# The k projection of the first attention half a row later, with its split and its stacking

## The chip, the cores and the metric

The kernel runs on one core of a Trainium2 chip. The metric is the device time of one execution, in microseconds (us), as the median of several runs.

## What is computed

Four layers follow each other on 8 sequences of 1024 tokens with 256 features: a causal attention with a window of 128 tokens, a mixture of experts that picks tokens, a linear attention, and a second full attention. Each adds its input and normalises the sum. The change touches the first attention alone:

```
q = apply_rope(proj(Wq, bq)) * Dh ** (-0.5)
k = apply_rope(proj(Wk, bk))
v = proj(Wv, bv)
scores = einsum('bhqd,bhkd->bhqk', q, k)
blocked = (rel > 0) | (rel < -WINDOW)
probs = softmax(where(blocked, -inf, scores))
out = einsum('bhqk,bhkd->bhqd', probs, v)
x = layernorm(x + einsum('bsd,ed->bse', out, Wo) + bo)
```

with 16 heads of 16 features.

## The kernel before

The first attention works in 16 blocks of 4 tiles of 128 tokens. Its engines run one hand-written list of steps, `steps` (lines 358 to 372), once for each block B; a step `(offset, kind, i)` works for block B + offset. Every engine takes its own part of each step in the order of the list, so the list sets the order on all five engines at once.

A pass through the list has four **rows**, i = 0 to 3. A row has two halves, and each half is made by `merged` (line 142), which places the j-th of n steps of a stream at the key (j + 0.5) / n and sorts all streams by that key; on equal keys the earlier stream goes first.

- First half: four weightings `pv` (probabilities times V, line 710), four score steps `nat` (scores whose row maximum is wanted, lines 775 and 785), and what `begun[i]` names. VectorE (DVE) reduces each `nat` to row maxima (line 655). Then `oT`, a copy of the weighted sum by ScalarE (ACT, line 601).
- Second half: four transposed score steps `tr` (lines 775 and 785 again), each of which ACT turns into exponentials (line 590); `maxT` (PE turns the row maxima, line 791, and DVE casts them, line 659); `place` (ACT issues two DMAs that put the maxima in place, line 596); `back` (line 794; DVE takes reciprocals and multiplies, lines 662 and 664); and what `front[i]` names: the projections `q`, `k` (both line 752) and `v` (line 757), the output projection `proj` (line 803, summed by DVE at line 671), `aoT` (transposes, line 798, copied by ACT at line 604), and the parts of the layer norm: `statistics` (lines 176 and 182, with the root on GpSimd, POOL, at line 189) and `normalise` (line 195).

PE writes the results of all steps in `slotted` to three PSUM slots of 1024 columns in turn (`Schedule`, line 260). A step waits until the step three places ahead of it in that ring has been read. Steps that have no block to work for are left out of the ring, as near the end of the layer.

The way of k: PE projects it (line 752), DVE adds the bias and multiplies by the rotation's tables in four instructions (line 639), POOL subtracts and adds (lines 549 and 551), ACT casts the high part (line 583) and POOL takes the low part (line 557); this is `split k`. SP then writes both parts to DRAM (line 507), and `stack k` reads them back in stacked form with six DMAs (line 481). The first `nat` of row 1 in the next pass waits for all of them (`stacked`, lines 727 to 729). POOL has `bias` (line 545) in row 2, between these steps. In the queue of SP, `normalise` stores the finished block (line 525), behind a wait for DVE's line 195.

`lent` (line 374) lists steps that stand empty in the last block; the next layer uses their slots to turn its first input (line 957) and to set up tables (`memsets`). The k projection is one of them: at its place DVE copies a turned tile and runs three memsets.

Of the kernel before, what the change touches and what calls it, by code (L numbers as in the profile page):

```python
# [338 lines left out]
def window_attention_layer(nc, block, semaphores, x_in, y_out, wq_in, wk_in, bq_in, bk_in, wvT, bv_in, woT, bo_in, cos_in, sin_in,  # L339
# [15 lines left out]
    SCALE = float(DH) ** -0.5  # L355
    CH = D // P

    begun = {1: [(2, "split q", 0)], 2: [(2, "split k", 0)], 3: [(2, "stack k", 0)]}
    front = {0: [(-1, "aoT", 1), (2, "xT", 0), (2, "xT", 1), (2, "q", 0)],
             1: [(2, "k", 0), (0, "again", 0)],  # L360
             2: [(0, "bias", 0), (-1, "proj", 0), (-1, "statistics", 0)],
             3: [(-1, "normalise", 0), (0, "aoT", 0), (1, "v", 0)]}
    steps = [(3, "load", 0)]
    for i in range(BT):
        on, tn = divmod(i + 3, BT)
# [10 lines left out]
    with ExitStack() as ctx:  # L376
# [3 lines left out]
        def part(buffer, first, shape, dtype=f32):  # L380

            n = 1
            for size in shape[1:]:
                n *= size
            names = "abcd"[:len(shape) - 1]
            flat = buffer[0:shape[0], first:first + n]
            flat = flat.rearrange(f"p ({' '.join(names)}) -> p {' '.join(names)}", **dict(zip(names[1:], shape[2:])))
            return flat if dtype == f32 else flat.bitcast(dtype)
# [23 lines left out]
        aoT = part(out_place, (CH + 2 + BT) * D, [P, CH, BW])  # L412
# [1707 lines left out]
def four_layers(nc, x, wq, wk, bq, bk, wv, bv, wo, bo, cos, sin, mask, maskT, ident, ident16,  # L2120
                controller, f1, f2, f1_bias, tie, wqkv, wproj, bproj, head_blocks,
                q_w, q_b, k_w, k_b, v_w, v_b, o_w, o_b, norm_w, norm_b, out):

    def dram(name, shape):
        return nc.dram_tensor(name, shape, f32, kind="Internal").ap()

    x1, x2, x3 = (dram(f"x{i}", (NSEQ, T, D)) for i in (1, 2, 3))
    with ExitStack() as counting, ExitStack() as opened:
        semaphores = Semaphores(nc, counting)
        with nc.Block() as block:  # L2130
            with ExitStack() as kept:
                first, programs = token_choice_layer(nc, block, semaphores, kept, x1, x2, controller, f1, f2, f1_bias, tie, ident,
                                                     dram("expert_outputs", (2, 128, 32, D)))
                tail = window_attention_layer(nc, block, semaphores, x, x1, wq, wk, bq, bk, wv, bv, wo, bo, cos, sin, mask, maskT, ident,
                                              ident16, dram("qk_rows", (2, 2, 2, 16, 2, 8, T // 2)), first)
                spent = tail.spent
                with ExitStack() as ctx:
                    tail = programs(tail, *allocators(nc, ctx, semaphores, "l0f")[:2])
            opening = Opening(*allocators(nc, opened, semaphores, "opening")[::2])
            tail = linear_attention_layer(nc, block, semaphores, tail, opening, x2, x3, wqkv, wproj, bproj, ident, head_blocks)  # L2140
            nested_width_attention_layer(nc, block, semaphores, spent, tail, opening, x3, out, q_w, q_b, k_w, k_b, v_w, v_b, o_w, o_b,
                                         norm_w, norm_b, dram("kq_rows", (2, 2, D, T)))
# [58 lines left out]
```

How the kernel before makes its waits and increments, by code:

```python
def wait_alone(eng, sem, value):  # L63
    eng.wait_ge(sem, value)
    alone(eng)
# [37 lines left out]
    def wait(self, eng, block, n=None):  # L103
        eng.wait_ge(self.sem, self.count(block, n))
# [27 lines left out]
    def wait_free(self, pe, b, key):  # L133
        old = self.before(key)
        if old is not None:
            for sem, per_sequence, position in self.emptied(old):
                pe.wait_ge(sem, b * per_sequence + position)
# [44 lines left out]
    def reciprocal_root(self, pool, b, use):  # L184
        pool.wait_ge(self.aggregated, self.count(b, use) * self.tiles)
        pool.tensor_scalar(self.mv[:, :, 1], self.mv[:, :, 1], LN_EPS, None, ALU.add).then_inc(self.var_ready, 1)
        pool.wait_ge(self.var_ready, self.count(b, use))
        pool.tensor_tensor(self.rstd[:, :], self.mv[:, :, 1], self.half[:, :], ALU.pow).then_inc(self.rstd_ready, 1)
# [45 lines left out]
    def wait_memsets(self, eng):  # L235
        eng.wait_ge(self.setup, 3)
# [15 lines left out]
def negative_mean(pool, ln, to, sems, X):  # L252
    pool.wait_ge(ln.rstd_ready, X + 1)
    pool.tensor_tensor(to[:, :], ln.mv[:, :, 0], ln.rstd[:, :], ALU.mult).then_inc(sems[0], 1)
    pool.wait_ge(sems[0], X + 1)
    pool.tensor_scalar(to[:, :], to[:, :], -1.0, None, ALU.mult).then_inc(sems[1], 1)
# [43 lines left out]
    def use(self, pe, X, step, B):  # L301
# [5 lines left out]
        if i > -4 * size:  # L307
            for sem, count in self.until(B + i // size, self.plan[i % size]):
                pe.wait_ge(sem, count)
        return self.slot_in(B, step)
# [649 lines left out]
    def logits(pe, X, s):  # L960
        if X == 0:
            pe.wait_ge(consts, 16 * NCONST)
        xT_even.wait(pe, X)
```

## Time and profile before

| | us |
|---|---|
| median of 3 runs | 2532.25 |
| lowest and highest | 2531.35, 2538.84 |
| the profiled execution | 2531.27 |
| its span, first to last instruction | 2529.4 |
| first attention, in that span | about 0 to 1060 |

| engine | busy us | share |
|---|---|---|
| PE | 2190.4 | 87% |
| DVE | 1419.5 | 56% |
| ACT | 994.7 | 39% |
| POOL | 899.1 | 36% |

The shares are averages over four layers. For this change only the first 1060 us count, and within them the repeating pass of about 61.7 us. The timeline gives for each instruction, or group of merged instructions, the start, the length, the engine and line, and in brackets the idle time before it with what ended it. Work of PE overlaps a little: the next piece can start up to 0.1 us before the last one is over.

### The profile page before, as it was taken

How to read it: one execution, taken by the hardware profiler on the slowest of the kernel's cores; microseconds unless marked ns; L12 is line 12 of the kernel's file. 1: busy time of each engine (PE TensorE's matmuls, PEld its weight loads, DVE VectorE, ACT ScalarE, POOL GpSimd, SP SyncE). 2: the span in 40 equal slices, each digit the busy share in tenths (PEclk: the TensorE clock that was granted, in tenths of full speed). 3: DMA queues.
4: the chain of work that ended last, by engine and by line, in shares of the span. 5: the costliest groups of instructions: out<-in, count | busy, mean ns of one | idle time of the engine just before them, and what ended most of it. 6: DMA issues, size and time to landing. Idle time of an engine off the chain costs nothing.

```text
span 2529.4 us, 42561 instructions
## 1 busy us (share of the span) xinstructions
PE 2190.4 (87%) x17140; PEld 1376.5 (54%) x17140; DVE 1419.5 (56%) x2526; ACT 994.7 (39%) x1450; POOL 899.1 (36%) x573
## 2 busy tenths in 40 slices
PE   4899999999999999788878599999588888888885
PEld 2445555555555555566667456776355555555553
DVE  3545555555555555556466444554466777676772
ACT  1233333333333333545435144333144554554443
POOL 4222222222222220103123022201457877787784
PEclk7899999999999999999999899999799999999997
DMA  6555555555555554367877722201663455445411
GB/s 150 117 118 110 109 110 110 109 115 110 113 110 116 110 107 89 125 212 261 280 248 266 263 92 67 67 26 33 190 161 99 114 145 145 132 113 146 128 35 50
DMA packets 227971, 328.81 MB, mean 130 GB/s; under 512 B 14544, under 2 KB 167104, under 8 KB 227520
## 3 DMA queue, kind: packets, MB, share of 16 engines
q1 hardware_dynamic: 220784, 321.49, 48.4%
q10 hardware_dynamic: 6992, 4.60, 0.6%
q8 instruction: 137, 2.24, 0.4%
q14 instruction: 58, 0.48, 0.1%
HBM read 197.46 MB, written 127.93 MB: 129 GB/s over the span
## 4 chain that ended last, share of the span: by engine, by line
PE 57%; DVE 16%; POOL 7%; DMA 7%; ACT 5%; issue 4%; SPq 3%; ACTq 1%; POOLq 0%; DVEq 0%
PE l0a_slot L775 8%; PE l0a_slot L785 7%; PE l0a_O L710 5%; DVE l1f_rowmax L1972 4%; PE l1a_slot L1568 4%; PE l0a_slot L752 4%; POOL l1f_added L1849 4%; ACT l0f_f L590 2%; PE l0a_slot L757 2%; PE l1a_slot L1559 2%; PE l0a_slot L803 2%; POOL l1f_added L1851 2%; DVE l0f_hidden L655 2%; DMA l0f_f<-in_dram 2%; PE l1f_slot L2103 2%
## 5 line engine op out<-in xcount | busy, mean ns | idle before, releaser
L590 ACT ACTIVATE l0f_f<-l0a_slot 128x1024 f32<-128x1024 f32 (+1 forms) x256 | 248.3, 971 | 337.8 <-PE l0a_slot L775 189.0
L655 DVE TENSOR_REDUCE l0f_hidden<-l0a_slot 128x4 f32<-128x1024 f32 (+1 forms) x256 | 293.4, 1156 | 115.5 <-PE l0a_slot L785 112.5
L1921 ACT ACTIVATE l1f_probs<-l1f_slot 128x1024 f32<-128x1024 f32 x240 | 243.8, 1022 | 271.9 <-PE l1f_slot L2103 265.2
L1849 POOL TENSOR_TENSOR l1f_added<-l1f_probs 128x1024 f32<-128x1024 f32 x117 | 277.3, 2370 | 152.4 <-ACT l1f_probs L1921 152.4
L1972 DVE TENSOR_REDUCE l1f_rowmax<-l1f_slot 128x1 f32<-128x1024 f32 x240 | 287.2, 1216 | 65.6 <-PE l1f_slot L2094 64.9
L775 PE MATMUL l0a_slot<-l0f_hidden 128*128 128x512 bf16 (+1 forms) x1024 | 296.0, 374 | 13.3 <-DMA l0f_hl<-qk_rows 9.0
L549 POOL TENSOR_TENSOR l0f_x<-l0f_x 128x512 f32<-128x512 f32 x32 | 40.7, 1272 | 540.3 <-DVE l0f_x L639 540.3
L2103 PE MATMUL l1f_slot<-l1f_Qs,l1f_Ks 128*128 128x256 f32 x960 | 173.9, 306 | 39.0 <-DVE l1f_lo L1962 14.8
L2103 PEld LDWEIGHTS l1f_slot<-l1f_Qs,l1f_Ks 128*128 128x128 f32 x960 | 146.3, 198 | 96.9 <-DVE l1f_rowmax L1972 33.9
L2094 PE MATMUL l1f_slot<-l1f_Ks,l1f_Qs 96*128 96x512 f32 x480 | 175.9, 451 | 25.7 <-DVE l1f_rowmax L1972 18.4
L710 PE MATMUL l0a_O<-l0f_f,l0f_wide 128*32 128x128 f32 x3840 | 156.4, 279 | 10.5 <-issue 10.5
L1851 POOL TENSOR_TENSOR l1f_added<-l1f_added 128x512 f32<-128x512 f32 x117 | 149.6, 1279 | 9.2
L2027 PE MATMUL l1f_os<-l1f_probs,l1f_V 128*32 128x256 f32 x1920 | 145.4, 396 | 0.1
L785 PE MATMUL l0a_slot<-l0a_Qs,l0f_hl 49*128 49x256 f32 (+1 forms) x1024 | 127.1, 327 | 18.3 <-ACT l0f_f L590 17.1
L785 PEld LDWEIGHTS l0a_slot<-l0f_hl,l0a_Qs 48*128 48x128 f32 x1024 | 77.7, 188 | 103.8 <-issue 103.8
L785 PEld LDWEIGHTS l0a_slot<-l0a_Qs,l0f_hl 49*128 49x128 f32 x1024 | 76.8, 186 | 103.3 <-issue 68.3
L752 PE MATMUL l0a_slot<-l0f_x,l0f_spread 128*128 128x512 f32 x256 | 123.5, 629 | 6.6 <-DVE l0f_spread L623 5.1
L785 PE MATMUL l0a_slot<-l0f_hl,l0a_Qs 48*128 48x256 f32 (+1 forms) x1024 | 128.7, 330 | 0.0
L710 PEld LDWEIGHTS l0a_O<-l0f_f,l0f_wide 128*32 128x32 f32 x3840 | 90.3, 109 | 64.6 <-issue 37.4
L775 PEld LDWEIGHTS l0a_slot<-l0f_hidden 128*128 128x128 bf16 x1024 | 63.8, 98 | 96.5 <-issue 61.7
L2094 PEld LDWEIGHTS l1f_slot<-l1f_Ks,l1f_Qs 96*128 96x128 f32 x480 | 78.3, 199 | 68.8 <-issue 30.0
L601 ACT COPY l0f_f<-l0a_O 128x512 f32<-128x512 f32 x64 | 37.4, 585 | 196.1 <-PE l0a_O L710 196.0
(194 smaller groups left out, 3770.2 us busy)
## 6 DMA issues: line engine op xcount, KB each, us to landing
expert_outputs<-l0f_wide SPq DMA_DIRECT2D x64, 512.0 KB, 3.3
l0f_wide<-expert_outputs SPq DMA_DIRECT2D x32, 1024.0 KB, 10.9
l1f_Ks<-kq_rows SPq DMA_DIRECT2D x48, 512.0 KB, 8.2
l0a_Qs<-qk_rows SPq DMA_DIRECT2D x90, 256.0 KB, 7.8
l0f_hl<-qk_rows SPq DMA_DIRECT2D x90, 256.0 KB, 14.5
l0f_f<-in_dram SPq DMA_DIRECT2D x10, 2048.0 KB, 14.7
qk_rows<-l0f_wide SPq DMA_DIRECT2D x32, 512.0 KB, 2.8
qk_rows<-l0f_x SPq DMA_DIRECT2D x32, 512.0 KB, 4.2
```

Source lines behind the costliest of these rows:

```text
L590: exp_ready.by(act.activation(probs[:, t % 2, HG * g:HG * g + HG, 0:reach, :], s[:, :, 0:reach, :], ACT.Exp, scale=SCALE))
L655: max_ready.by(dve.reduce_max(rowmax[:, t, :, 2 * g:2 * g + 2], s[:, :, :, first:2 * P], AX))
L710: last = mm(O[t % 2][32 * j:32 * j + 32, g, :], V[:, tile - a, HG * g + j, :], probs[:, (t - a) % 2, HG * g + 2 * (j % 2) + j // 2, a, :], ...
L752: last = mm(s[:, BW * r:BW * r + BW], w[:, c, P * r:P * r + P], xT[:, n, c, :], start=c == 0, stop=c == CH - 1)
L775: at_end = mm(o[:, half, :, reach, :], ident16[:, :], table[:, reach, :].unsqueeze(1).broadcast_to([P, 2, wide, P]), start=not mask_ends, ...
L785: last = mm(o[:, half, j, reach, :].rearrange("p a q -> p (a q)"), left[r, 2 * g + j, here], right[r, 2 * g + j, moving], start=mask_ends ...
L1849: halved.by(pool.tensor_tensor(added[:, u, :], probs[:, 0, u, :], probs[:, 1, u, :], ALU.add))
L1851: add_done.by(pool.tensor_tensor(added[:, u, 0:SKT * QW], added[:, u, 0:SKT * QW], added[:, u, SKT * QW:HKT * QW], ALU.add))
L1921: exp_done.by(act.activation(probs[:, half, u - FIRST[b], :], s[:, :], ACT.Exp, scale=SCALE))
L1972: max_done.by(dve.reduce_max(rowmax[:, i:i + 1], s[:, :], AX))
L2094: last = mm(s[:, 512 * half:512 * half + 512], Qs[0:96, parity, u, P * t:P * t + P], Ks[0:96, parity, UNITS[u][0], 512 * half:512 * half + ...
L2103: last = mm(s[:, QW * j:QW * j + QW], Ks[:, parity, UNITS[u][0], P * kt:P * kt + P], Qs[:, parity, u, :], start=True, stop=True)
```

## The change

```
-    begun = {1: [(2, "split q", 0)], 2: [(2, "split k", 0)], 3: [(2, "stack k", 0)]}
+    begun = {1: [(2, "split q", 0)], 2: [(2, "k", 0)]}
     front = {0: [(-1, "aoT", 1), (2, "xT", 0), (2, "xT", 1), (2, "q", 0)],
-             1: [(2, "k", 0), (0, "again", 0)],
-             2: [(0, "bias", 0), (-1, "proj", 0), (-1, "statistics", 0)],
-             3: [(-1, "normalise", 0), (0, "aoT", 0), (1, "v", 0)]}
+             1: [(0, "again", 0)],
+             2: [(0, "bias", 0), (2, "split k", 0), (-1, "proj", 0), (-1, "statistics", 0)],
+             3: [(-1, "normalise", 0), (2, "stack k", 0), (0, "aoT", 0), (1, "v", 0)]}
```

The k projection moves from the second half of row 1 to the first half of row 2 (the third row), `split k` from the first to the second half of row 2, and `stack k` from the first to the second half of row 3. Since `merged` places a stream's steps by their number, the streams of rows 2 and 3, now of four steps each, also put their other steps elsewhere: `proj` comes after the third `tr` instead of the second; `normalise` comes ahead of `maxT`; `aoT` comes after the third `tr`; and `v` comes behind the fourth `tr`, as the last step of the pass.

**DVE, rows 1 and 2.** Line 639 with `l0a_bk` is the taking of k, line 655 reduces a `nat`, line 659 casts the maxima. Before:

```order
L639 SCALAR_TENSOR_TENSOR l0f_x<-l0a_slot2,l0a_bk,l0f_spread 128x512 [waits l0a_lo_ready,l0a_hi_ready,l0a_filled3]
L639 SCALAR_TENSOR_TENSOR l0f_x<-l0a_slot2,l0a_bk,l0f_spread 128x512 x3
L662 RECIPROCAL l0f_hidden<-l0a_slot2 128x16 [waits l0a_filled1]
L664 TENSOR_TENSOR l0f_f2<-l0a_slot2,l0f_hidden 128x256 [waits l0a_recip_ready]
L655 TENSOR_REDUCE l0f_hidden<-l0a_slot1 128x2x2 [waits l0a_filled2]
L655 TENSOR_REDUCE l0f_hidden<-l0a_slot2 128x2x2 [waits l0a_filled2]
L655 TENSOR_REDUCE l0f_hidden<-l0a_slot0 128x2x2 [waits l0a_filled2]
L655 TENSOR_REDUCE l0f_hidden<-l0a_slot1 128x2x2 [waits l0a_filled2]
L659 CAST l0f_hidden<-l0a_slot0 16x128 [waits l0a_placed1,l0a_filled2]
```

Now:

```order
L662 RECIPROCAL l0f_hidden<-l0a_slot1 128x16 [waits l0a_filled1]
L664 TENSOR_TENSOR l0f_f2<-l0a_slot1,l0f_hidden 128x256 [waits l0a_recip_ready]
L655 TENSOR_REDUCE l0f_hidden<-l0a_slot0 128x2x2 [waits l0a_filled2]
L655 TENSOR_REDUCE l0f_hidden<-l0a_slot1 128x2x2 [waits l0a_filled2]
L639 SCALAR_TENSOR_TENSOR l0f_x<-l0a_slot2,l0a_bk,l0f_spread 128x512 [waits l0a_lo_ready,l0a_hi_ready,l0a_filled3]
L639 SCALAR_TENSOR_TENSOR l0f_x<-l0a_slot2,l0a_bk,l0f_spread 128x512 x3
L655 TENSOR_REDUCE l0f_hidden<-l0a_slot0 128x2x2 [waits l0a_filled2]
L655 TENSOR_REDUCE l0f_hidden<-l0a_slot1 128x2x2 [waits l0a_filled2]
L659 CAST l0f_hidden<-l0a_slot0 16x128 [waits l0a_placed1,l0a_filled2]
```

The taking of k stands between the second and the third reduction of row 2, where it stood ahead of row 1's `back`.

**PE, end of row 3.** Line 798 is `aoT`, 794 is `back`, 757 is `v`, lines 775 and 785 are a `tr`, 710 is the first weighting of the next pass. Before:

```order
L798 MATMUL l0a_slot1<-l0f_ident,l0f_f2 128x128 [waits l0a_exp_ready,l0a_ao_ready]
L798 MATMUL l0a_slot1<-l0f_ident,l0f_f2 128x128 x3
L775 MATMUL l0a_slot2<-l0f_hidden 128x512 [waits l0a_maxT_ready]
L775 MATMUL l0a_slot2<-l0f_hidden 128x512
L785 MATMUL l0a_slot2<-l0a_Qs,l0f_hl 128x256 x4
L794 MATMUL l0a_slot0<-l0f_ident,l0f_f2 128x128 [waits l0a_exp_ready,l0a_oT_ready]
L794 MATMUL l0a_slot0<-l0f_ident,l0f_f2 128x128 x3
L757 MATMUL l0a_slot1<-l0f_spread,l0f_x 128x256 [waits l0a_aoT_ready]
L757 MATMUL l0a_slot1<-l0f_spread,l0f_x 128x256 x7
L785 MATMUL l0a_slot2<-l0a_Qs,l0f_hl 128x256 [waits l0a_exp_ready]
L785 MATMUL l0a_slot2<-l0a_Qs,l0f_hl 128x256 x3
L775 MATMUL l0a_slot2<-l0f_hidden 128x512 x2
```

Now:

```order
L775 MATMUL l0a_slot1<-l0f_hidden 128x512
L785 MATMUL l0a_slot1<-l0a_Qs,l0f_hl 128x256 x4
L798 MATMUL l0a_slot2<-l0f_ident,l0f_f2 128x128 [waits l0a_maxT_ready,l0a_ao_ready]
L798 MATMUL l0a_slot2<-l0f_ident,l0f_f2 128x128 x3
L794 MATMUL l0a_slot0<-l0f_ident,l0f_f2 128x128 [waits l0a_exp_ready,l0a_oT_ready]
L794 MATMUL l0a_slot0<-l0f_ident,l0f_f2 128x128 x3
L785 MATMUL l0a_slot1<-l0a_Qs,l0f_hl 128x256 [waits l0a_exp_ready]
L785 MATMUL l0a_slot1<-l0a_Qs,l0f_hl 128x256 x3
L775 MATMUL l0a_slot1<-l0f_hidden 128x512 x2
L757 MATMUL l0a_slot2<-l0f_spread,l0f_x 128x256 [waits l0a_aoT_ready]
L757 MATMUL l0a_slot2<-l0f_spread,l0f_x 128x256 x7
L710 MATMUL l0a_O0<-l0f_f1,l0f_wide 32x128 [waits l0a_oT_ready,l0a_v_ready,l0a_exp_ready]
```

`v` has changed places with the last `tr`, and two of the `tr` steps now use slot 1 with only `aoT` and `back` between them.

**DVE, row 3.** Line 195 is `normalise`, line 659 the cast of the maxima that `place` waits for. Before:

```order
L655 TENSOR_REDUCE l0f_hidden<-l0a_slot0 128x2x2 [waits l0a_filled2]
L659 CAST l0f_hidden<-l0a_slot2 16x128 [waits l0a_placed0,l0a_filled2]
L195 TENSOR_SCALAR l0f_x<-l0f_x,l0a_ln_mv,l0a_ln_rstd 128x256 [waits l0a_ln_rstd_ready]
L195 TENSOR_SCALAR l0f_x<-l0f_x,l0a_ln_mv,l0a_ln_rstd 128x256 x3
L662 RECIPROCAL l0f_hidden<-l0a_slot0 128x16 [waits l0a_filled1]
L664 TENSOR_TENSOR l0f_f2<-l0a_slot0,l0f_hidden 128x256 [waits l0a_recip_ready]
L647 TENSOR_TENSOR l0f_wide<-l0a_slot1,l0f_f2 128x16x16 [waits l0a_pv_done,l0a_filled2]
```

Now:

```order
L655 TENSOR_REDUCE l0f_hidden<-l0a_slot0 128x2x2 [waits l0a_filled2]
L195 TENSOR_SCALAR l0f_x<-l0f_x,l0a_ln_mv,l0a_ln_rstd 128x256 [waits l0a_ln_rstd_ready]
L195 TENSOR_SCALAR l0f_x<-l0f_x,l0a_ln_mv,l0a_ln_rstd 128x256 x3
L659 CAST l0f_hidden<-l0a_slot2 16x128 [waits l0a_placed0,l0a_filled2]
L662 RECIPROCAL l0f_hidden<-l0a_slot0 128x16 [waits l0a_filled1]
L664 TENSOR_TENSOR l0f_f2<-l0a_slot0,l0f_hidden 128x256 [waits l0a_recip_ready]
L647 TENSOR_TENSOR l0f_wide<-l0a_slot2,l0f_f2 128x16x16 [waits l0a_pv_done,l0a_filled2]
```

`normalise` stands ahead of the cast. On SP's queue, in words: the store of the finished block (line 525) now stands ahead of the six stacking DMAs of k, and was behind them.

## Rows read from the trace of the kernel before

**Rows 1.** Busy time in stretches: start:end, length, PE, PEld, DVE, ACT, POOL, clock, DMA.
```profile
60.00:121.70 61.70, 54.11 (x321) 25.92 (x319) 30.61 (x39) 15.47 (x17) 11.96 (x8) 0.86 0.65 131
...
430.00:491.60 61.60, 57.29 (x504) 31.25 (x500) 34.02 (x54) 20.91 (x26) 13.37 (x9) 1.00 0.56 112
```

**Rows 2.** Waits of PE, us 121.7 to 1007.3: total us, times, longest us.
```profile
PE l0a_slot L785 <- ACT l0f_f L590: 15.4, 29, 1.1
PE l0a_slot L791 <- DVE l0f_hidden L655: 15.0, 37, 0.6
PE l0a_slot L794 <- DVE l0f_x L639: 14.0, 13, 1.1
PE l0a_O L710 <- issue: 9.3, 15, 1.1
```

**Rows 3.** Timeline, PE, rows 1 and 2: start, length, instructions, idle before.
```profile
419.80 3.60 PE L752 MATMUL l0a_slot<-l0f_x,l0f_spread 128*128 128x512 f32 x8
...
426.31 0.63 PE L794 MATMUL l0a_slot<-l0f_ident,l0f_f 128*128 128x128 f32 x4 [1.07 <-DVE l0f_x L639]
...
435.42 0.28 PE L791 MATMUL l0a_slot<-l0f_ident,l0f_hidden 128*16 128x128 f32 x1 [0.63 <-DVE l0f_hidden L655]
...
475.35 0.65 PE L710 MATMUL l0a_O<-l0f_f,l0f_wide 128*32 128x128 f32 x16
475.93 0.60 PE L775 MATMUL l0a_slot<-l0f_hidden 128*128 128x512 bf16 x2
...
476.90 0.64 PE L710 MATMUL l0a_O<-l0f_f,l0f_wide 128*32 128x128 f32 x16
```

**Rows 4.** Timeline, PE, row 3 and the next block's start.
```profile
449.42 0.28 PE L791 MATMUL l0a_slot<-l0f_ident,l0f_hidden 128*16 128x128 f32 x1 [0.35 <-DVE l0f_hidden L655]
...
451.89 0.66 PE L794 MATMUL l0a_slot<-l0f_ident,l0f_f 128*128 128x128 f32 x4
452.68 3.72 PE L757 MATMUL l0a_slot<-l0f_spread,l0f_x 128*128 128x256 f32 x16
...
457.95 0.43 PE L710 MATMUL l0a_O<-l0f_f,l0f_wide 128*32 128x128 f32 x8 [0.59 <-issue]
```

**Rows 5.** Timeline, DVE, rows 3, 0 and 1.
```profile
448.14 1.22 DVE L655 TENSOR_REDUCE l0f_hidden<-l0a_slot 128x4 f32<-128x1024 f32 x1 [0.32 <-PE l0a_slot L785]
449.74 0.28 DVE L659 CAST l0f_hidden<-l0a_slot 16x128 fp32r<-16x128 f32 x1 [0.37 <-PE l0a_slot L791]
449.94 1.36 DVE L195 TENSOR_SCALAR l0f_x<-l0f_x,l0a_ln_mv,l0a_ln_rstd 128x256 f32<-128x256 f32 x4
...
456.44 1.41 DVE L647 TENSOR_TENSOR l0f_wide<-l0a_slot,l0f_f 128x256 f32<-128x256 f32 x4 [3.13 <-PE l0a_slot L757]
...
473.91 2.73 DVE L639 SCALAR_TENSOR_TENSOR l0f_x<-l0a_slot,l0a_bq,l0f_spread 128x512 f32<-128x512 f32 x4 [4.38 <-PE l0a_slot L752]
476.56 4.77 DVE L655 TENSOR_REDUCE l0f_hidden<-l0a_slot 128x4 f32<-128x1024 f32 x4
```

**Rows 6.** Timeline, ACT and its DMA queue, row 3.
```profile
450.70 1.02 ACT L590 ACTIVATE l0f_f<-l0a_slot 128x1024 f32<-128x1024 f32 x1 [0.57 <-PE l0a_slot L775]
450.71 1.29 ACTq L596 DMA_DIRECT2D l0a_Qs<-l0f_hidden  x2
452.04 0.58 ACT L604 COPY l0f_f<-l0a_slot 128x512 f32<-128x512 f32 x1 [0.31 <-issue]
```

**Rows 7.** Timeline, SP's queue, row 3; then landing times of line 481's transfers.
```profile
446.50 3.77 SPq L481 DMA_DIRECT2D l0f_hl<-qk_rows  x6
451.38 0.36 SPq L525 DMA_DIRECT2D x<-l0f_x  x1
...
DMA to landing us min/median/max: 4.5/11.2/18.1
```

**Rows 8.** Timeline, PE, last two blocks of the first attention.
```profile
973.23 0.50 PE L785 MATMUL l0a_slot<-l0a_Qs,l0f_hl 49*128 49x256 f32 x4 [0.49 <-ACT l0f_f L590]
...
1033.24 0.38 PE L775 MATMUL l0a_slot<-l0f_hidden 128*128 128x256 bf16 x2 [1.90 <-DVE l0f_f L664]
```

## The prediction

> **What bounds the kernel now.** I read the busy time in stretches first. In the settled part of the first attention PE is busy 57.29 of 61.60 us at a granted clock of 1.00, DVE 34.02, ACT 20.91, POOL 13.37 [rows 1]. So PE sets the time of a pass of the step list, and only what makes PE idle can be won or lost: about 4.3 us a pass. The waits of PE say where these are [rows 2]. Four kinds carry nearly all: PE waits for ACT's exponentials (15.4 us in 29 waits), with `maxT` for DVE's row maxima (15.0 in 37), with `back` for the taking of k (14.0 in 13), and at the first weighting (9.3 in 15; the page says "issue", but line 710 there waits for V, and DVE's line 647 ends just before it). Then I read the timeline around these places. The same pass comes back 14 times almost to the tenth, so one instance stands for all.
>
> The reader is to see one more thing in the timeline: work that ends a wait is covered only by the PE work that stands between. The change moves one step on purpose and several others by the rule of `merged`, so each wait has to be worked out anew from what now stands ahead of it.
>
> **Row 1: the wait behind k goes.** Before, k ends at 423.40, DVE takes it for 2.73 us, PE fills only two `tr` in that time and then `back`, which uses the slot of k, sits idle 1.07 us [rows 3]. Without k in that row, `back` uses the slot of `maxT`, whose cast is over long before. The `tr` steps behind `maxT` then wait for exponentials of the one two places ahead at the earliest; ACT needs 1.02 us for one [rows 6] and PE 0.97, with `maxT` or `back` between, so nothing is left over. k stands in 14 settled passes (blocks 0 to 13): **-1.07 x 14 = -15.0 us**.
>
> **Row 2: `maxT` waits longer.** k now ends between the second and third `nat`. I take its follow-up from q, which DVE takes at the start of a row in the same way: 2.73 us from 473.91, then four reductions in 4.77, so 1.19 each when they queue [rows 5]. Two of them make 2.4, and `maxT` can start about 0.05 + 2.7 + 2.4 + 0.05 = 5.2 us after k ends. In that time PE has two weightings and two `nat` of 1.55 together (475.35 to 476.90) of which the weighting is 0.58 (475.35 to 475.93) [rows 3], and one `tr` of the same 0.97: 3.1 + 0.97 = 4.07. The idle time is 1.14 where it is 0.35 in a usual row [rows 4]. In every second pass the `tr` is a narrow one, about 0.8; there it is 1.3 against 0.63 [rows 3]. So +0.79 and +0.68 in turn, **7 x 0.79 + 7 x 0.68 = +10.3 us**. The POOL and ACT parts of k (1.27 twice, a cast of 1.04, 2.35 for the low part, with 2.36 of `bias` now ahead of it) run while PE does the third `tr` and `proj`, 3.5 us, and nobody waits for them; I cost them at nothing. Without that cover they would cost at most the cast, 1 us a pass. `proj` behind the third `tr` moves DVE's sum and statistics about 1 us towards the next row; its first reduction starts some 0.7 us late and DVE, with 1.22 of work for every 1.55, has caught up by the third. Nothing again.
>
> **Row 3: V comes too late for the next weighting.** Before, `v` ends at 452.68 + 3.72 = 456.40, DVE starts at 456.44 and is done at 457.85, and the weighting starts at 457.95, 1.55 after the end of `v`; the last `tr` covers 0.96 of it and 0.59 is idle [rows 4, 5]. Now `v` is the last step and covers nothing: the whole 1.55 is idle, 0.96 more. `v` exists in 16 passes: **16 x 0.96 = +15.4 us**.
>
> **Row 3: the last `tr` waits for an exponential.** It uses the slot of the `tr` before it, with only `aoT` and `back` between. The same four steps (`maxT`, two `tr`, `aoT`) stand ahead of `back` as before, so `back` still runs from 451.89 to 452.55 [rows 4]. ACT is what has changed. It has to issue `place` between the exponentials, and `place` waits for the cast of the maxima, which now stands behind `normalise` on DVE: reduction to 449.36, `normalise` 1.36, cast 0.28, so 451.00 [rows 5]. The two DMAs take 1.29 and the next ACT instruction started 0.04 behind them [rows 6]: 452.34, then the exponential from 452.4 to 453.4, and the last `tr` at 453.45. That is 0.9 us idle, against 0.13 ahead of `v` before (452.55 to 452.68 [rows 4]): +0.77 in 14 passes, **+10.8 us**. If ACT does not let `place` hold it up, its end is 0.35 sooner and the term is +0.42 x 14 = 5.9; if the slot is free in time after all it is -0.13 x 14 = -1.8. I take the 0.77, since the rows show ACT's next instruction waiting for the DMA's end.
>
> **The two ends of the layer.** In the last blocks k, q and xT have nothing to do. Before, two `tr` of block 14 share a slot because k's place between them is empty: 0.49 idle, which goes. In the last block DVE runs the memsets at k's place and PE waits 1.90 for the `back` behind them; half a row later they lie beside `proj` and cost nothing [rows 8]. **-2.4 us**. At the start PE fills and waits in long stretches, at 0.86 of its clock in the first passes [rows 1]; I see no price there, and allow 3 us either way.
>
> **The sum** is -15.0 + 10.3 + 15.4 + 10.8 - 2.4 = +19.1 us against the profiled execution of 2531.27, so 2550.4. The median of the runs is 1.0 above that execution, so **2551 us**, 0.75% slower.
>
> **Rival 1: the smaller price.** `place` and the slot in row 3 cost nothing: without the +10.8 and with -1.8 it is 2532.25 + 6.5 = 2539. For it speaks that a few tenths of drift between ACT and PE decide; against it that ACT's chain adds up to nearly 1 us more than PE has to do. The decision point is an exponential that ends before 452.55.
>
> **Rival 2: faster.** Only the removed waits count (-15.0, -2.4) and the new places of `v`, `maxT` and the last `tr` are absorbed: 2532.25 - 17.4 = 2515. That needs PE to have later work that it may do first; the order shows PE's queue as a fixed list in which the weighting waits for V, so little speaks for it.
>
> **Rival 3: the stacked k lands too late.** SP's store waits for `normalise` (issued at 451.38) and now stands ahead of the six DMAs of k, which were issued from 446.50 on [rows 7]. They start 5 us later at least, at about 452, and are read by the first `nat` of row 1, some 0.6 after q's end at 473.9, or 2 us later in the new pass: 24 us. The longest landing is 18.1 us [rows 7]. Half of the queue ahead of them (q's share) will be further along, so I expect landings of no more than 18. Beyond a margin of 6 us each further microsecond costs 14 us; with 3 of them it is 2551 + 42 = 2593. The Trainium skill ("DMA: Bandwidth & Descriptors", section on queues, rings and completion order) says that each DMA engine consumes the descriptors of one queue in ring order; by that rule the 512 KB of the store also go ahead of k. The landing times of 18.1 us against an issue of 3.77 us for six agree with a queue that is worked off in turn.
>
> **Rival 4: the clock falls.** With some 1.4 us more idle time in a pass, and two waits close together in row 3, the granted clock could leave 2.4 GHz for stretches. In the early pass at a mean of 0.86, PE is at the lower level for 28% of 61.7 us and does 8.6 us less work at full speed [rows 1]. Were each pass to lose as much, it would be 2551 + 14 x 8.6 = 2671. Against it: the waits of today, 4.3 us a pass with single ones of 1.07, leave the clock at 1.00 [rows 1, 3]. The Trainium skill ("TensorE: Matmul & The Clock Gate", section on PSUM-queue depth-cycling) tells of a kernel whose clock swung because PE was idle for short times between groups while it turned through its PSUM banks. This kernel turns through three slots with waits of that kind, and its rows at 1.00 so far do not show it.
>
> **How the numbers follow.** A measurement of this kernel can tell about 0.3% from no change, 7.6 us. My forecast has 0.77, rival 1 with its kin (one of the three costs in rows 2 and 3 missing) 0.11, rival 2 0.05, rival 3 0.05, rival 4 0.02. Rival 1 at 2539 counts as no change. The range takes the forecast with its bounds (the `tr` term between 5.9 and 12, `maxT` 3 us either way, the start 3) and reaches to rival 1: 2539 to 2561. Faster 0.05, within 0.3% 0.12, slower 0.83.
>
> **What would show it.** In the profile after: no wait of line 794 for line 639; `maxT` of row 2 waiting 1.1 to 1.3 us; the first weighting of a pass waiting 1.5; line 785 of row 3 waiting 0.9 for line 590; a pass of about 63.1 us in place of 61.7; PE's clock still 1.00; no wait for the stacking. It is wrong if the pass is 61.7 or less, or if the stacked k or the clock appears among the causes.

## The result and the profile after

| | before | after |
|---|---|---|
| median, us | 2531.8 | 2571.55 |
| lowest and highest | 2530.9, 2538.84 | 2562.66, 2573.58 |
| the profiled execution | 2531.27 | 2573.58 |
| its span | 2529.4 | 2571.7 |

The changed kernel takes 1.0139 times as long (95% interval 1.012 to 1.0159), 39.8 us more by the medians. The forecast was 2551 with a range of 2539 to 2561: the direction was right, the loss is twice what was forecast and lies outside the range. Two single executions further down (3104 and 3491 us) ran at a much lower clock from start to end, and the medians given are those of the other executions.

The two spans, cut at the first and the sixteenth `v` and at the first turned tile of the second layer. The columns are start:end, length, busy time and count of PE, PEld, DVE, ACT and POOL, then clock and DMA. Before:

```profile
0.00:83.86 83.86, 46.96 (x142) 20.95 (x142) 35.40 (x37) 9.55 (x11) 33.49 (x18) 0.76 0.65 152
83.86:1002.06 918.20, 857.38 (x7682) 470.02 (x7680) 487.67 (x773) 323.41 (x386) 189.74 (x127) 1.00 0.54 107
1002.06:1058.39 56.33, 45.90 (x499) 30.21 (x500) 28.14 (x46) 24.26 (x29) 5.42 (x4) 0.98 0.40 139
1058.39:2529.40 1471.01, 1240.15 (x8820) 855.34 (x8820) 868.32 (x1672) 637.49 (x1025) 670.41 (x425) 0.94 0.46 142
```

After:

```profile
0.00:87.94 87.94, 50.27 (x148) 22.61 (x149) 36.84 (x37) 10.58 (x12) 33.53 (x18) 0.72 0.64 147
87.94:1041.63 953.69, 869.70 (x7681) 477.63 (x7680) 480.45 (x774) 321.59 (x385) 189.78 (x127) 0.98 0.52 104
1041.63:1096.35 54.72, 44.93 (x495) 29.46 (x493) 27.51 (x44) 23.38 (x28) 5.26 (x4) 1.00 0.37 128
1096.35:2571.70 1475.35, 1235.94 (x8820) 853.49 (x8820) 866.37 (x1672) 637.74 (x1025) 671.01 (x425) 0.94 0.47 142
```

Of the 42.3 us between the spans, 35.5 lie in the passes (953.69 - 918.20), 4.1 ahead of the first `v`, -1.6 behind the last, and 4.3 in layers whose code is the same. In the passes PE is idle for 84.0 us in place of 60.8, **+23.2**, and it is busy for 869.7 in place of 857.4 with as many instructions, **+12.3**. The forecast had the first of these two numbers and not the second.

The waits of PE after, from 121.7 to 1030 us (total us, times, longest), beside the same rows of before [rows 2]:

```profile
PE l0a_slot L785 <- ACT l0f_f L590: 31.8, 43, 1.2
PE l0a_slot L791 <- DVE l0f_hidden L655: 24.0, 36, 1.3
PE l0a_O L710 <- issue: 21.8, 14, 1.6
```

The row of line 794 behind line 639 is gone (-14.0). Line 785 has 16.4 more, line 791 9.0 more, line 710 12.5 more: +23.9 in all. The same places in the timeline of PE, one narrow pass, beside [rows 3, 4]:

```profile
452.27 0.28 PE L791 MATMUL l0a_slot<-l0f_ident,l0f_hidden 128*16 128x128 f32 x1 [1.30 <-DVE l0f_hidden L655]
...
468.65 0.60 PE L794 MATMUL l0a_slot<-l0f_ident,l0f_f 128*128 128x128 f32 x4
470.41 0.50 PE L785 MATMUL l0a_slot<-l0a_Qs,l0f_hl 49*128 49x256 f32 x4 [1.16 <-ACT l0f_f L590]
...
471.28 3.62 PE L757 MATMUL l0a_slot<-l0f_spread,l0f_x 128*128 128x256 f32 x16
476.46 0.42 PE L710 MATMUL l0a_O<-l0f_f,l0f_wide 128*32 128x128 f32 x8 [1.56 <-issue]
```

And where PE is busy for longer. The pass that follows, PE's timeline behind `maxT` of row 2:

```profile
515.60 0.28 PE L791 MATMUL l0a_slot<-l0f_ident,l0f_hidden 128*16 128x128 f32 x1 [1.02 <-DVE l0f_hidden L655]
515.81 0.50 PE L785 MATMUL l0a_slot<-l0a_Qs,l0f_hl 49*128 49x256 f32 x4
516.25 1.61 PE L775 MATMUL l0a_slot<-l0f_hidden 128*128 128x512 bf16 x4
517.78 0.79 PE L785 MATMUL l0a_slot<-l0a_Qs,l0f_hl 49*128 49x256 f32 x4
518.50 4.43 PE L803 MATMUL l0a_slot<-l0f_f 128*128 128x256 f32 x16
```

and the same stretch in windows (columns as above, the clock third from the end):

```profile
512.00:516.00 4.00, 2.98 (x33) 1.47 (x33) 3.63 (x5) 1.61 (x2) 3.91 (x3) 1.00 0.00 0
516.00:520.00 4.00, 4.00 (x16) 2.20 (x15) 0.20 (x1) 2.88 (x3) 1.88 (x2) 0.57 0.01 2
520.00:524.00 4.00, 4.00 (x24) 3.16 (x22) 1.02 (x1) 0.00 (x0) 1.42 (x1) 1.00 0.42 155
```

About one microsecond behind the end of a wait of 1.02 the granted clock goes from 2.4 to 1.2 GHz (the mean of 0.57 over 4 us puts the change at 516.6), stays there for about 3.4 us, and the four instructions that took 0.50 take 0.79. In windows of 2 us the trace of after has seven such **falls** between 130 and 1030 us: at 137, 196 (a long one, 7 us), 517, 544, 773, 838 and 967. Each begins within 2.0 us of the end of a wait that the change made: five behind `maxT` of row 2 (1.02 or 1.30), one behind the wait of 1.14 of line 785, one behind the 1.55 at the first weighting. Summed as (1 - clock) x length, which I call the **shortfall**, they come to 13.7 us. The trace of before has none there, in 15 waits of 1.02 and more.

### The profile page after: what moved, and what is told of

Read it like the earlier page. It is cut to its first block, busy times and chain, and to the rows that moved or that the text cites. A ratio compares the mean times of both kernels' runs of the same rounds, so it can differ in the third digit from the quotient of the medians.

```text
span 2571.7 us, 42561 instructions
## 1 busy us (share of the span) xinstructions
PE 2200.8 (86%) x17140; PEld 1383.2 (54%) x17140; DVE 1411.2 (55%) x2526; ACT 993.3 (39%) x1450; POOL 899.6 (35%) x573
## 4 chain that ended last, share of the span: by engine, by line
PE 56%; DVE 15%; DMA 7%; POOL 7%; ACT 6%; issue 4%; SPq 3%; ACTq 1%; POOLq 0%; DVEq 0%
PE l0a_slot L775 8%; PE l0a_slot L785 7%; PE l0a_O L710 5%; DVE l1f_rowmax L1972 4%; PE l1a_slot L1568 4%; PE l0a_slot L752 4%; POOL l1f_added L1849 4%; ACT l0f_f L590 4%; DMA l0f_f<-in_dram 2%; PE l0a_slot L803 2%; PE l0a_slot L757 2%; DVE l0f_hidden L655 2%; PE l1a_slot L1559 2%; POOL l1f_added L1851 2%; PE l0f_slot L1274 2%
```

## The experiments

The kernels below place single steps at keys of their own. `merged` got a second list for it, and with the keys of before or after it gives their order again:

```
def merged(*streams, at=()):
    ...
    keyed += [(key, 9, step) for key, step in at]
```

In the expectations `maxT` and `tr` go by the number of the step: "row 1's `maxT`" is step `maxT` 1, which stands in row 2. "Passes" is the time from the first to the sixteenth `v` in the trace. The medians of before differ from chip to chip (2534 to 2537 here, 2531.8 above), so each forecast is best read against the before of its own chip.

**k, its split and its stacking alone** (the keys of the other steps as before).

```
-    begun = {..., 2: [(2, "split k", 0)], 3: [(2, "stack k", 0)]}
+    begun = {..., 2: [(2, "k", 0)]}
+    front: 1: 0.5 again;  2: 1/6 bias, 0.375 split k, 0.5 proj, 5/6 statistics
+           3: 1/6 normalise, 0.375 stack k, 0.5 aoT, 5/6 v
```

> k, its split and its stacking stand where the change puts them; bias, proj, statistics, normalise, aoT and v keep the places of before. Theory A (the loss is idle time of PE that the neighbours' new places cause, and a clock that falls where such waits follow each other): the wait behind k goes (-15.0 us), the wait of maxT in row 2 stays at 1.0 to 1.3 us (+10 us), row 3 is as before, so 2522 to 2532 us, and the clock falls in one or two passes at most. Theory B (moving k itself, its DMAs above all, is what costs): it stays near 2565.

Measured: 2534.96 against 2535.59 of before on that chip, ratio 0.9995 (0.9978 to 1.0011). The wait behind k is gone, line 791 waits 24.4 us in 37 in place of 15.0, and PE's idle time in the passes falls from 60.8 to 55.3; one fall of the clock, behind a `maxT` wait of 1.30 at 804, takes 1.7 back. The row of line 785 stays at 16.3 us in 30, so neither k nor its stacking beside row 3 makes the wait of the last `tr`. The median lies 3 us above the stated 2522 to 2532, on a chip where before is 3 us slower too. What the change's title names costs nothing that can be measured, and theory A holds.

**Row 3 alone** (k where it was, row 3 as the change has it).

```
-             3: [(-1, "normalise", 0), (0, "aoT", 0), (1, "v", 0)]}
+             3: 0.125 normalise, 0.375 stack k, 0.625 aoT, 0.875 v
```

(`stack k` leaves the first half of row 3 for it.)

> Before with only row 3 of the change: stacking of k in its second half, normalise ahead of maxT, aoT behind the third tr, v last; k and its split where they were before. Theory A: the last tr waits 1.16 us instead of 0.13, and the first weighting 1.56 instead of 0.59, so 14 x 1.03 + 16 x 0.97 = +30 us from the waits, 2562 us, and more where the clock falls. Theory B: about 2532, since k is not moved.

Measured: 2569.59, 34.0 more than before on that chip where some 30 were expected, ratio 1.0131 (1.0104 to 1.0158). Its waits:

```profile
PE l0a_slot L785 <- ACT l0f_f L590: 31.5, 43, 1.2
PE l0a_O L710 <- issue: 21.8, 14, 1.6
PE l0a_slot L794 <- DVE l0f_x L639: 15.1, 14, 1.1
```

Nearly the whole loss is here, by two waits that the k projection itself has nothing to do with: `stack k` is a fourth step in `front[3]` and pushes the three others off their keys (in the next two kernels `v` and `normalise` are told apart). Two falls, both behind a wait of 1.56, add 3.4.

**`v` last alone** (before, with the key of `v` from 5/6 to 0.9).

> The kernel before with one step in another place: v of the next block behind the last tr of row 3, not ahead of it. By the sum on record the wait behind v grows from 0.59 to 1.55 (0.96 in 16 passes, +15.4); the last tr, no longer behind v, comes 3.5 us earlier and waits for its slot if ScalarE's copy is not done. Theory A (aoT's and stack k's place costs nothing of itself): 2547 to 2552 with no wait of the last tr, up to 2568 with a wait of 1.2 there as in the kernel with row 3 alone. Theory B (stack k beside it makes the last tr's wait): 2547 to 2552. What tells them apart is the row of L785 behind ScalarE's L590: 15.4 us in 29 waits as before for B, 31 in 43 for A.

Measured: 2555.59 against 2536.89, +18.7, ratio 1.0085 (1.0063 to 1.0107). Line 710 waits 23.4 us in 15, up to 1.6, and line 785 still 15.4 in 29. So `v` behind the last `tr` costs its 0.97 a pass in idle time, and the last `tr`'s wait is not its doing. That much is theory B; that `stack k` itself makes the wait, as B puts it, is not what the next kernel shows. Here the last `tr` uses the slot of `aoT` and waits 0.2 us in all for its copy. Three falls, behind waits of 1.56 at 462.5, 527.2 and 779.6, add 5.1 us of shortfall.

**The cast ahead of `normalise`** (after, `normalise` from 0.125 to 0.17).

> The changed kernel with normalise behind row 3's maxT, where the kernel before has it, and all else as changed. VectorE then casts maxT first. If the last tr waits for ScalarE, whose copies stand behind what VectorE gives it, the wait of 1.16 becomes about 0.8 and the kernel some 5 us faster than the changed one: 2564 to 2568; fewer stretches at the lower clock would add up to 5. If ScalarE's own work between sets that wait, nothing moves: 2570 to 2573. By neither does the wait behind v (1.56) change.

Measured: 2569.58, ratio 1.0134 (1.0118 to 1.015), no faster than after. But the wait is shorter, as expected. ACT and its queue in row 3, first in the kernel after, where VectorE's cast ends at 467.53:

```profile
467.56 1.66 ACTq L596 DMA_DIRECT2D l0a_Qs<-l0f_hidden  x2
469.33 1.02 ACT L590 ACTIVATE l0f_f<-l0a_slot 128x1024 f32<-128x1024 f32 x1 [0.91 <-issue]
```

and with the cast first:

```profile
465.50 1.29 ACTq L596 DMA_DIRECT2D l0a_Qs<-l0f_hidden  x2
466.89 1.02 ACT L590 ACTIVATE l0f_f<-l0a_slot 128x1024 f32<-128x1024 f32 x1 [0.37 <-issue]
...
467.97 0.51 PE L785 MATMUL l0a_slot<-l0a_Qs,l0f_hl 49*128 49x256 f32 x4 [0.62 <-ACT l0f_f L590]
```

The last `tr` waits 0.62 for 1.16, line 785 in all 24.1 us for 31.8. This shows the chain that the prediction named (cast, two DMAs of `place`, exponential, `tr`). The 0.62 that is left belongs to the new place of `aoT`: the last `tr` uses the slot of the `tr` before it, whose exponential ends at 467.91. Of the 7.7 us, 5.1 came back as clock in this trace: eight falls, 18.8 us of shortfall in place of 13.7, so that the passes are 4.1 us shorter and not 9; the later layers took 5.4 us longer in this execution. The stated 2564 to 2568 was missed for that.

The two DMAs took 1.29 us here and 1.66 in after, and SP's queue shows a difference beside them. In after they start with the stacking of k:

```profile
467.42 0.36 SPq L525 DMA_DIRECT2D x<-l0f_x  x1
467.88 4.29 SPq L481 DMA_DIRECT2D l0f_hl<-qk_rows  x6
```

With the cast first they begin 1.1 us ahead of SP's line 481 (466.63). In row 3 of after and of row 3 alone, all 25 such pairs lie beside 1.5 us or more of SP's DMA issuing and take 1.7 us; with the cast first and with k alone, all 26 lie beside 0.5 us of it and take 1.3. That the issuing of SP holds up that of ACT is likely by this, and was not tested by itself.

**The first `nat` of row 0 ahead of the first weighting** (after, streams exchanged).

```
-        steps += merged([... "pv" ...], [... "nat" ...], begun.get(i, []))
+        steps += merged(nats, pvs, begun.get(i, [])) if i == 0 else merged(pvs, nats, begun.get(i, []))
```

> The changed kernel with row 0's first nat ahead of its first pv, so that the nat (0.9 us of TensorE work that needs no V) covers the wait for VectorE's V. If V's arrival is what the idle behind v is, it falls from 1.56 to about 0.6: 0.95 in 14 to 16 passes, 15 us, and fewer falls of the clock, up to 7 more: 2549 to 2558. Rival: nat waits itself there for a slot or for the stacked k or q, and the idle only moves: 2566 to 2574. A second rival: ScalarE and VectorE, which then get row 0's work in another order, hold up the rest of the row: 2575 to 2590.

Measured: 2560.76, ratio 1.0098 (1.0082 to 1.0115). Line 710 waits 9.7 us in 14, longest 0.7, in place of 21.8, so it is V that the first weighting waits for. The passes are 12.2 us shorter than after, all of it idle time; there are still seven falls, now all behind the 1.30 of `maxT`. So the gain in the passes is the wait's own 12, without the fewer falls that the stated 2549 to 2558 counted on. All seven waits of 1.30 have a fall behind them here, six of seven with the cast first, and one of seven with k moved alone: the length of the wait does not decide by itself.

**All three waits filled with short matmuls** (after).

```
+            def busy(X, count, o, times):
+                oT_ready.wait(pe, X, count)
+                for m in range(times):
+                    mm(O[o][:, 0:2, :], ident16[:, :], mask[:, :, :], start=True, stop=True, ...)
...
+                if kind == "maxT" and i == 1 and 1 <= B < NBLOCK - 2:
+                    busy(X - 1, 2, 1, 5)
+                if kind == "tr" and i == NHG - 1 and 1 <= B < NBLOCK - 1:
+                    busy(X - 1, 3, 0, 6)
...
+                if kind == "v" and 1 <= B < NBLOCK - 1:
+                    busy(X - 1, 3, 0, 8)
```

> The changed kernel, with short bf16 matmuls of 256 columns written ahead of the three waits that the change made longer: 5 ahead of row 1's maxT, 6 ahead of row 3's last tr, 8 behind v (into bank halves of O that are free there; no result is read). At 0.11 us each (256 columns at 2.4 GHz) they are 0.5, 0.6 and 0.9 us in waits of 1.3, 1.2 and 1.6, so they should end before the wait does and cost nothing by themselves. Theory A (waits of one microsecond and more, close together, let the clock fall, and that is what the sum of the waits lacked): each wait in the trace is shorter by what was written into it, no stretch at 0.5 of the clock between 130 and 1000 us, and the 12.6 us that those stretches cost in the profiled passes are gone: 2556 to 2562. Theory B (the falls have another cause, or cost nothing of their own): the falls stay, 2568 to 2576. If TensorE's own time in these matmuls is longer than I reckon, the passes grow by the excess, at most 2600.

Measured: 2562.25, ratio 1.0101 (1.0082 to 1.012); its interval overlaps that of after only at the very edge. One narrow pass of its trace (line 700 is the filling; the others moved down by nine):

```profile
448.23 0.72 PE L700 MATMUL l0a_O<-l0f_hidden 128*128 128x256 bf16 x5
449.60 0.28 PE L800 MATMUL l0a_slot<-l0f_ident,l0f_hidden 128*16 128x128 f32 x1 [0.65 <-DVE l0f_hidden L655]
...
472.07 1.04 PE L700 MATMUL l0a_O<-l0f_hidden 128*128 128x256 bf16 x8
473.79 0.43 PE L719 MATMUL l0a_O<-l0f_f,l0f_wide 128*32 128x128 f32 x8 [0.68 <-issue]
```

The filling and the wait that is left are 1.37 together (0.72 + 0.65) where the wait was 1.30, and 1.72 (1.04 + 0.68) where it was 1.56: no useful work is added or taken away. Undisturbed passes are 62.57 and 64.15 us, as in after (62.55 and 64.15). Yet the passes take 943.4 in place of 953.7, because six of the seven falls are gone: theory A. The one that is left is a long one and begins at 134, behind the `maxT` of block 0, which was left unfilled:

```profile
133.15 0.28 PE L800 MATMUL l0a_slot<-l0f_ident,l0f_hidden 128*16 128x128 f32 x1 [1.02 <-DVE l0f_hidden L655]
133.35 0.50 PE L794 MATMUL l0a_slot<-l0a_Qs,l0f_hl 49*128 49x256 f32 x4
133.79 1.61 PE L784 MATMUL l0a_slot<-l0f_hidden 128*128 128x512 bf16 x4
```

An earlier filling, with 24, 28 and 36 f32 matmuls of 128 columns at the same waits, decides nothing:

> The changed kernel with small extra matmuls into the free accumulator at the three long waits (24 ahead of maxT in row 2, 28 ahead of the last tr, 36 behind v; 16 of this kind take 0.58 us in a weighting), so that PE works where it was idle and no step starts later. Theory A with the clock: the stretches at the lower clock go from blocks 1 to 14, and it is 12 to 17 us faster than the changed kernel, 2554 to 2560. Theory without a clock (the whole 40 us are waits): it is the same as the changed kernel or slower, 2571 or more.

Measured: 2648.34, ratio 1.0427 (1.039 to 1.0464). The trace has two records for each of these f32 matmuls (48, 56 and 72), and they lasted up to 2.8 us, longer than the waits. Beside that six new waits of 2.3 to 4.5 us came, about 140 us apart and in the middle of a weighting (line 717):

```profile
570.18 0.43 PE L717 MATMUL l0a_O<-l0f_f,l0f_wide 128*32 128x128 f32 x8
575.12 0.66 PE L717 MATMUL l0a_O<-l0f_f,l0f_wide 128*32 128x128 f32 x8 [4.52 <-issue]
```

No other engine works in most of that time (ACT's last exponential is over at 561.25, VectorE's reduction at 571.5). What PE waits for there stays open; the DMA queue of instructions carries 156 packets in place of the 137 of after.

**One kind of wait filled.** First only the wait behind `v` (the last two added lines above):

> The changed kernel with only the 8 short matmuls behind v (1.04 us of the wait of 1.56 in the trace with all three waits filled); row 1's maxT still waits 1.30 and the last tr 1.16. Theory A: the falls behind maxT stay, 4 to 7 of them, 2566 to 2572. Rival (the longest wait makes the falls): none or one is left, 2556 to 2563.

Measured: 2572.48, ratio 1.0153 (1.013 to 1.0176). Five falls, as theory A had it: three behind `maxT` waits of 1.30 and 1.02, one behind the `maxT` of block 0, one at 157 behind the one 1.56 that stands ahead of the first filled block. Then only `maxT` (the first two added lines):

> The changed kernel with only the 5 short matmuls ahead of row 1's maxT (0.72 us of its wait of 1.30 in the trace with all three waits filled); the last tr's 1.16 and the 1.56 behind v stay idle. Theory A (a fall of the clock follows one long wait, and the wait of row 1's maxT is the one that starts most of them, as it is in the trace with nat first): 2 to 4 falls are left between 130 and 1030 us, those behind v, as in the kernel with v last alone (3): 5 us of shortfall in place of 13.7, 2561 to 2566. Rival (the falls need the wait behind v, the longest): 6 or 7 falls stay, 2569 to 2575.

Measured: 2568.02, ratio 1.0135 (1.0115 to 1.0154). The mean clock of its trace is 0.64, in which single falls can't be seen. The same kernel once more:

> The same kernel as the one with only row 1's maxT filled, whose profiled execution was disturbed and told nothing of its falls. With all three waits filled one fall was left, with only the wait behind v filled five, all but one of them right behind a maxT's wait of 1.30. Theory A (the 1.30 of maxT starts most falls): 1 to 3 falls between 130 and 1030 us, with a shortfall of 2 to 5 us, and 2561 to 2568. Rival (any of the three long waits will do, so that it takes all three to be filled): 4 to 7 falls, now behind the waits of 1.56 and 1.16, and 2568 to 2574.

Measured: 2565.27, ratio 1.0119 (1.0097 to 1.0142). Three falls, two of them long, 8.6 us of shortfall: one behind the unfilled `maxT` of block 0, the two others behind waits of 1.56. One of these, with the windows from 596 to 608:

```profile
599.47 0.43 PE L717 MATMUL l0a_O<-l0f_f,l0f_wide 128*32 128x128 f32 x8 [1.56 <-issue]
...
601.15 0.91 PE L782 MATMUL l0a_slot<-l0f_hidden 128*128 128x512 bf16 x2
602.00 0.79 PE L792 MATMUL l0a_slot<-l0f_hl,l0a_Qs 48*128 48x256 f32 x4
```

```profile
596.00:600.00 4.00, 2.44 (x18) 1.63 (x17) 1.42 (x4) 0.00 (x0) 0.00 (x0) 1.00 1.11 207
600.00:604.00 4.00, 4.00 (x30) 1.40 (x28) 2.39 (x2) 0.00 (x0) 0.00 (x0) 0.66 1.07 153
604.00:608.00 4.00, 4.00 (x21) 1.46 (x20) 1.90 (x3) 0.59 (x1) 0.00 (x0) 0.50 1.08 155
```

Whichever wait is filled, no fall is left behind it, and the waits left open still have some. Theory A was right on the number of falls (1 to 3) and the time, and wrong on the shortfall (2 to 5 us); that the falls left stand behind waits of 1.56 is what the rival said.

**`v` earlier, and both steps where their waits have cover** (before, with `v` at 0.6, ahead of the third `tr`; then also k at 0.9, behind the last `tr` of row 1).

```
-             1: [(2, "k", 0), (0, "again", 0)],
+             1: 0.75 again, 0.9 k
-             3: [(-1, "normalise", 0), (0, "aoT", 0), (1, "v", 0)]}
+             3: 1/6 normalise, 0.5 aoT, 0.6 v
```

> The kernel before with one step in another place: v of the next block ahead of the third tr of row 3, not ahead of the last. By the rule that a step of 3.7 us that stands late in the row lets VectorE's V come late, the wait of 0.59 behind v goes: 0.59 in 15 passes, 9 us, and nothing is late in its place: 2522 to 2528. If the slot of the third tr is late then (its copy by ScalarE), 2528 to 2534.

Measured: 2526.73 against 2534.05, ratio 0.997 (0.9959 to 0.9982): as expected. In the passes the row of line 710 is down to 0.2 us from 9.9, and line 775 has 2.4 of new waits. Behind the passes, at 1019.5, the clock falls once, behind a wait of 1.91 that before has too (1.90 in [rows 8]), there without a fall.

> Before with k as the last step of row 1 (behind the fourth tr, as q stands in row 0) and v between the second and third tr of row 3; split and stacking where they were. Theory A: the 1.07 us behind k go (14 times) and the 0.59 us ahead of the first weighting go (16 times), 24 us in all, so about 2508 us. If taking k late only moves its wait to maxT of row 2, about 2520.

Measured: 2516.47 against 2535.59, ratio 0.9926 (0.9908 to 0.9943), 19.1 less than before on that chip and the fastest kernel here. Of the 24 us that were expected the idle time of the passes gives 16.6 (44.2 for 60.8), and there is no fall. k itself now waits, by 5.2 us in 7, and line 775 by 3.9 in 8. One wait of k is 0.73, behind an exponential that `place` holds up:

```profile
353.42 1.93 ACTq L596 DMA_DIRECT2D l0a_Qs<-l0f_hidden  x2
355.45 1.94 ACT L590 ACTIVATE l0f_f<-l0a_slot 128x1024 f32<-128x1024 f32 x2 [1.01 <-PE l0a_slot L794]
...
356.53 3.70 PE L752 MATMUL l0a_slot<-l0f_x,l0f_spread 128*128 128x512 f32 x8 [0.73 <-ACT l0f_f L590]
```

**The traces in one table** (us; the long waits are those of 1.0 and more of a settled pass, by kind; falls and shortfall from 130 us to the last `v`):

| kernel | long waits of a settled pass | falls | passes | shortfall | passes less shortfall |
|---|---|---|---|---|---|
| before | 1.07 | 0 | 918.2 | 0 | 918.2 |
| k moved alone | 1.02/1.30 | 1 | 916.4 | 1.7 | 914.7 |
| row 3 alone | 1.07, 1.16, 1.56 | 2 | 946.4 | 3.4 | 943.0 |
| `v` last alone | 1.07, 1.56 | 3 | 934.2 | 5.1 | 929.1 |
| after | 1.02/1.30, 1.16, 1.56 | 7 | 953.7 | 13.7 | 940.0 |
| cast first | 1.02/1.30, 1.56 | 8 | 949.6 | 18.8 | 930.8 |
| `nat` first | 1.02/1.30, 1.16 | 7 | 941.5 | 13.7 | 927.8 |
| all filled | none | 1 | 943.4 | 3.4 | 940.0 |
| behind `v` filled | 1.02/1.30, 1.16 | 5 | 947.6 | 8.5 | 939.1 |
| `maxT` filled, again | 1.16, 1.56 | 3 | 947.6 | 8.6 | 939.0 |
| `v` earlier | 1.07 | 0 | 906.8 | 0 | 906.8 |
| both | none | 0 | 901.2 | 0 | 901.2 |

The four kernels that differ only in filling come to 939.0 to 940.0 once the shortfall is taken off. So a fall costs its shortfall in full, within the 1 us by which they differ.

The waits of 1.02 and more between 130 us and the last `v`, in the same twelve traces:

| wait | times | with a fall behind it |
|---|---|---|
| `maxT` of row 2, 1.30 | 35 | 19 |
| `maxT` of row 2, 1.02 | 36 | 7 |
| first weighting, 1.55 to 1.56 | 72 | 10 |
| last `tr`, 1.14 to 1.19 | 68 | 1 |
| `back` behind k, 1.07 to 1.08 | 53 | 0 |
| others, 1.06 to 1.43 | 17 | 0 |

A wait of 1.02 ahead of `maxT` has a fall behind it seven times, a wait of 1.07 ahead of `back` never. So length alone does not choose. What else takes part stays open; no kernel here was made to find it out.

## Why the prediction was wrong

- **Row 1, the wait behind k** (-15.0): right. The row is gone, -14.0 in the window shown.
- **Row 2, `maxT`** (+10.3, waits of 1.14 and 1.3): right. 1.02 and 1.30, +9.0.
- **Row 3, V** (+15.4, a wait of 1.55): right. 1.55 and 1.56. The rows say +12.5 in a window that holds 14 of them, where the row of before also has one wait of 1.09 of another cause; 14 times 0.97 is 13.6.
- **Row 3, the last `tr`** (+10.8, a wait of 0.9): the chain is right, as the cast-first kernel shows; the size is short. The two DMAs of `place` took 1.66 us here, beside SP's stacking of k, not the 1.29 of [rows 6], and the wait is 1.16: +16.4 in place of 10.8. It is the term whose size is furthest off.
- **The ends** (-2.4, start within 3): -1.6 behind the last `v`, +4.1 ahead of the first, where PE's clock is 0.72 for 0.76. Both hold a shift of the boundary, since the last `tr` (six matmuls) now stands ahead of `v`; only their sum counts.
- **POOL, ACT and statistics at nothing; stacked k in time (rival 3)**: right. No wait of PE for POOL or for a DMA stands among those of the passes after. The longest landing was 19.2 us, 1.2 more than expected and well inside the margin of 6.
- **The clock.** This is the step that failed: the sum adds only idle time of PE and has no term for the clock, which it takes to stay at 1.00. "What would show it" asks for 1.00 and calls the forecast wrong if the clock is among the causes; it is 0.98 in the passes, and PE is busy for 12.3 us more with as many instructions. Without these 12.3 the measured 2571.55 would lie inside the range. Rival 4 named the mechanism and got a chance of 0.02, with a price (8.6 us for every pass, 2671) that left nothing between 0 and 120 us. The argument against it was that single waits of 1.07 leave the clock alone [rows 1, 3]; it did not say what a 1.3 or a 1.56 would do. That argument was true of the waits of 1.07 behind k (53 in twelve traces, no fall) and did not carry over to others of like length. What the runs show is a mechanism that acts now and then: seven falls of 1.7 to 3.4 us of shortfall in 14 passes. The Trainium skill ("TensorE: Matmul & The Clock Gate", section on PSUM-queue depth-cycling) describes PE idle for short times between groups of matmuls and the throughput lost to it. The trace of after agrees: its waits are of 1.56 us at most, its clock falls seven times, and 13.7 us are lost.

In numbers, for the span: the four terms of the passes were forecast at +21.5 and idle time rose by 23.2; the ends were forecast at -2.4 and came to +2.5; the clock added 12.3 in the passes. The 4.3 us of the later layers are not the change's by any row I found: with the same code these layers take between 1471.0 and 1481.4 us in the thirteen undisturbed traces here, of kernels that differ only in the first attention, and the 1471.0 of before is the lowest. With the 13.7 us of shortfall as a term the forecast would have been about 2565. The pass without a fall was forecast at 63.1 us; wide and narrow ones take 64.15 and 62.55, 63.35 in the mean.

What stays open: which of the long waits starts a fall. In after, the same `maxT` wait of 1.30 at 452.27 has no fall behind it and the one at 836.87 has. Before, the waits of 1.07 never had one in the passes. Runs of one kernel differ in it too, probably (after ranges over 11 us in four runs), but only one execution of each was traced.

## What to carry to other kernels

A step moved into a merged list moves its neighbours: here the moved k costs nothing that can be measured and the neighbours that were pushed off their places (`v`, `normalise`, `aoT`) cost nearly everything, so read each queue's new order step by step and ask for every PE step what it now waits for and what covers the wait. Where PE sets the time, a new wait of one to one and a half microseconds can have a second price beside its length; look at the granted clock behind it in short windows, and give it a chance and a size of its own. Rows of waits elsewhere in the kernel that leave the clock alone do not show that the new ones will. A step whose result comes back through another engine (k, v) belongs ahead of PE work that does not need it, as in the kernel with both moved.

## What the runs showed of the hardware

- In the twelve traces of the table all 37 falls begin 0.1 to 2.1 us behind the end of a PE wait of 1.02 us or more; no other wait of 0.3 or more stands between. Most such waits have no fall (281 with 37 in all; after has 43 with 7, before 15 with none), and the share differs by the place of the wait: 19 of 35 for the `maxT` waits of 1.30, none of 53 for the waits of 1.07 behind k. A short fall costs 1.7 us and a long one 3.4, more than the wait itself.
- Matmuls of 256 bf16 columns whose result nobody reads, put into the waits, removed six of seven falls: 10.3 us of the passes came back, for some 2.6 us of filling in each pass that took the place of idle time.
- The pair of small DMAs that ACT issues in `place` took 1.29 us (before), 1.66 (after) and 1.93 (both moved) in the rows shown, and ACT's next instruction started 0.04 to 0.11 us behind its end each time. The 1.7 of row 3 goes with SP issuing DMAs at the same time.
